# Two cross-attention layers on one core: the last two batch entries drained together, four orders changed in the repeated step

## The reference

```python
# layer 0, 16 heads of 16: only the context rows within 1 of each token's index count
q = split(rmsnorm(x, gamma_q) @ Wq.T); kn = rmsnorm(ctx, gamma_kv)
k, v = split(kn @ Wk.T), split(kn @ Wv.T)
w = square(relu(einsum('bhqd,bhkd->bhqk', q, k) / 4)); w = where(mask, w, 0)
x = x + merge(einsum(w / maximum(w.sum(-1), 1e-6), v)) @ Wo.T
# layer 1, one head
q, k, v = gelu(x @ Wq + bq), gelu(ctx @ Wk + bk), gelu(ctx @ Wv + bv)
x = softmax(q @ k.T) @ v @ Wf + bf + x
out = (x - mean) * rsqrt(var + 1e-5) * ln_gamma + ln_beta
```

## Time and profile before

| | |
|---|---|
| median of 3 runs | 367.44 us (366.91 to 369.47) |
| profiled execution | 368.78 us, of which the profile's span is 367.0 us |
| PE busy | 339.8 us, 93% |
| VectorE busy | 309.7 us, 84% |
| ACT busy | 246.3 us, 67% |
| POOL busy | 179.8 us, 49% |
| time of the chain that ended last | PE 66%, DVE 10%, ACT 9%, POOL 8% |
| mean granted clock of PE | 0.974 of 2.4 GHz |

### The profile page before, as it was taken

How to read it: one execution, slowest core, us unless ns; L and a number is a source line. 1 busy time by engine, 2 the same in 40 slices (tenths; PEclk the granted TensorE clock), 3 DMA queues, 4 the chain that set the end, 5 groups by cost and what they waited for, 6 DMA issues and landing times.

```text
span 367.0 us, 5550 instructions
## 1 busy us (share of the span) xinstructions
PE 339.8 (93%) x1904; PEld 241.2 (66%) x1904; DVE 309.7 (84%) x486; ACT 246.3 (67%) x491; POOL 179.8 (49%) x218
## 2 busy tenths in 40 slices
PE   3989998999999999999999999999999999978871
PEld 1565767767676767676767676767676767656740
DVE  0879696999998989998999999999999999895635
ACT  3797423477777686868686868686959595838542
POOL 3715020026565655556564747473838383636153
PEclk9989999999999999999999999999999999998985
DMA  7965625804141413132323232222222321101003
GB/s 245 325 193 143 198 67 127 246 2 142 57 144 58 143 60 136 65 126 75 117 84 114 86 108 94 101 96 95 91 102 81 101 89 49 59 0 57 2 0 114
DMA packets 21946, 38.48 MB, mean 105 GB/s; under 512 B 2144, under 2 KB 8288, under 8 KB 21920
## 3 DMA queue, kind: packets, MB, share of 16 engines
q1 hardware_dynamic: 18800, 29.48, 25.3%
q0 software_dynamic: 2160, 7.87, 6.2%
q10 hardware_dynamic: 960, 0.79, 0.7%
HBM read 17.29 MB, written 8.39 MB: 70 GB/s over the span
## 4 chain that ended last, share of the span: by engine, by line
PE 66%; DVE 10%; ACT 9%; POOL 8%; issue 7%; ACTq 0%; POOLq 0%
PE ps L440 9%; PE ps L442 8%; PE ps L441 8%; PE ps L519 8%; PE ps L485 6%; ACT bufs L880 4%; PE ps L675 4%; PE ps L569 4%; PE ps L491 4%; PE ps L684 4%; DVE stats L1111 4%; PE ps L600 4%; PE ps L574 2%; POOL rstd L379 2%; PE ps L472 1%
## 5 line engine op out<-in xcount | busy, mean ns | idle before, releaser
L1042 DVE TENSOR_TENSOR qkp<-ps,bufs 128x1024 f32<-128x1024 f32 x48 | 55.8, 1213 | 2.4 <-PE ps L485 2.4
L350 POOL TENSOR_TENSOR x_lo<-x_ring,x_hi 128x1024 fp32r<-128x1024 f32 x16 | 38.3, 2395 | 39.8 <-ACT x_hi L842 39.8
L389 POOL TENSOR_TENSOR bufs<-bufs,lng_row 128x1024 f32<-128x1024 f32 x15 | 36.1, 2404 | 36.9 <-ACT bufs L880 34.9
L918 ACT ACTIVATE xp_hi<-bufs 128x512 fp32r<-128x512 f32 x30 | 18.9, 632 | 50.5 <-DVE bufs L1122 50.5
L1053 DVE TENSOR_TENSOR ps<-ps,wn 128x1024 f32<-128x1024 f32 x32 | 39.2, 1224 | 2.8 <-PE ps L491 2.8
L363 POOL TENSOR_TENSOR mean_gap<-stats 128x4 f32<-128x4 f32 x14 | 2.8, 197 | 71.1 <-DVE stats L1111 71.1
L391 POOL TENSOR_TENSOR bufs<-bufs,lnb_row 128x1024 f32<-128x1024 f32 x15 | 35.6, 2374 | 1.2
L519 PE MATMUL ps<-qkp,cst 128*32 128x512 f32 x192 | 30.7, 598 | 0.4 <-DVE qkp L1042 0.4
L519 PE MATMUL ps<-bufs,cst 128*32 128x512 f32 x64 | 30.5, 598 | 0.0
L880 ACT ACTIVATE bufs<-ps,nbias,rstd 128x256 f32<-128x256 f32 x56 | 28.5, 568 | 2.7 <-POOL nbias L380 2.4
L440 PE MATMUL ps<-xp_hi,wh_q 128*128 128x512 f32 (+1 forms) x68 | 27.6, 405 | 2.6 <-DVE xp_lo L1125 1.9
(11 more groups left out here) (205 smaller groups left out, 925.8 us busy)
## 6 DMA issues: line engine op xcount, KB each, us to landing
x_ring<-xT SPq DMA_DIRECT2D x16, 512.0 KB, 3.5
out<-bufs POOLq DMA_DIRECT2D x15, 512.0 KB, 3.5
idx_ring<-idx SPq DMA_DIRECT2D x16, 256.0 KB, 4.0
wkv_lo<-kv SPq DMA_DIRECT2D x32, 126.0 KB
kvs<-kv SPq DMA_DIRECT2D x30, 126.0 KB
vfd<-bufs SPq DMA_DIRECT2D x8, 256.0 KB, 4.1
qkp<-ctxT SPq DMA_DIRECT2D x2, 512.0 KB, 7.3
bufs<-ctx SPq DMA_DIRECT2D x2, 512.0 KB, 8.7
```

Of the source, the lines that this page charges most:

```text
L350: G.tensor_tensor(x_lo[:, :, :], x_ring[:, e % RING, :, :], f32_view(x_hi[:, :, :]), ALU.subtract).then_inc(xl_ready, 2)
L389: G.tensor_tensor(zo, zn, lng_row[:, :].unsqueeze(1).broadcast_to([P, TT, D]), ALU.mult).then_inc(zg_ready, 1)
L1042: V.tensor_tensor(qk[:, s, :, :], ps[:, bank0:bank0 + 2, :], q0, ALU.mult).then_inc(qk_ready, 1)
```

## The change

**In the repeated step.** POOL no longer doubles `half_rstd` into `rstd`; ACT scales with `half_rstd`, `nbias` uses half of the shift's factor, and gamma is doubled once (`lng_twice`). ACT normalises all four tiles before it copies the second half of q0 (it did two, the copy, two). PE makes the second queries from the half `c = 1` first and waits for each half's rounding apart. PE starts the scores when the first half's gelu is done. These last two waits were one wait for both halves each.

**In the drain.** The step's loop ends one step earlier (`s` = 16). A list written out by hand takes its place and the old drain's: entry 14 (`OLD`) and entry 15 (`LAST`) alternate. The last picked values of 15 stand ahead of 14's second queries; 15's third product and sum are done in halves in VectorE (`half_third`); the halves of 15 use buffers and PSUM banks of their own and stand among 14's scores, exponentials and outputs. Products of the halves do their high parts first and wait for the remainder only then. POOL makes the remainder of half 1, VectorE rounds half 1. The scores of a half are packed as two tiles of 64 by 128, with one transpose each. The norms of 14 and 15 come last: statistics by VectorE; for 15, VectorE subtracts the mean and multiplies gamma in PSUM, then scales and adds beta; for 14, ACT normalises, then POOL does gamma and beta of one pair of tiles and VectorE those of the other, whose normalised rows stay in PSUM. SP issues four transfers of 256 KB. ACT's table loads are forced early by a one-element activation.

```diff
@@ gpsimd, norm_factors and scale_rows
-                G.tensor_scalar(nmean2[:, :], mean2[:, :], -1.0, None, ALU.mult).then_inc(mean_ready, 1)
+                G.tensor_scalar(nmean2[:, :], mean2[:, :], -0.5, None, ALU.mult).then_inc(mean_ready, 1)
-                G.tensor_tensor(rstd[:, :], half_rstd[:, :], half_rstd[:, :], ALU.add).then_inc(nbias_ready, 1)
+                    G.tensor_tensor(lng_twice[:, :], lng_row[:, :], lng_row[:, :], ALU.add).then_inc(twice_ready, 1)
@@ gpsimd, after the loop
+            norm_factors(OLD - 1)
+            scale_rows(OLD - 1)
+            write_rows(OLD - 1)
+            half_remainder(1)
+            final_power(0)
+            final_bias(0)
+            final_power(1)
+            final_gamma(0, 0)
+            final_beta(0, 0)
@@ tensor, step
-                    for c in range(DC):
-                        product(ps[:, Q1_BANKS[i], :], *weight("q1", c, i), xp_hi[:, c, :], xp_lo[:, c, :], c == 0, c == DC - 1, q1_mm)
+                    for c in (1, 0):
+                        if i == 0:
+                            pe.wait_ge(xph_ready, 2 * b + (2 - c))
+                            pe.wait_ge(xpl_ready, 2 * b + (2 - c))
+                        product(ps[:, Q1_BANKS[i], :], *weight("q1", c, i), xp_hi[:, c, :], xp_lo[:, c, :], c == 1, c == 0, q1_mm)
-                    pe.wait_ge(xph_ready, 2 * b + 2)
-                    pe.wait_ge(xpl_ready, 2 * b + 2)
@@ scalar, step (the two halves of normalise)
                 if n is not None:
                     normalise(range(2, TT))
+                if n is not None:
+                    normalise(range(0, 2))
                 if a is not None and f is not None:
...
                     copy_q0(a, 1)
-                if n is not None:
-                    normalise(range(0, 2))
@@ vector, after the loop: the product of a half, and the norm
+            def half_third(h):
+                dve.wait_ge(vg_mm, 3 * LAST + 3)
+                V.tensor_tensor(ps[:, 2 + h, :].rearrange("p (x d) -> p x d", d=HD), ps[:, 2 + h, :].rearrange("p (x d) -> p x d", d=HD),
+                                wn[:, CENTRE, 2 * h:2 * h + 2, :].rearrange("p j h -> p (j h)").unsqueeze(2).broadcast_to([P, 2 * H, HD]),
+                                ALU.mult).then_inc(half_prod, 1)
+                dve.wait_ge(half_prod, h + 1)
+                dve.wait_ge(sum_ready, 2 * LAST + 1)
+                V.tensor_tensor(att_flat(0)[:, h, :], ps[:, 2 + h, :], att_flat(1)[:, h, :], ALU.add).then_inc(half_sum, 1)
+            def final_centred(m, h):
...
+                    last = V.scalar_tensor_tensor(z, z, fin_nmean_t[:, m, j:j + 1], lng_row[:, :], ALU.add, ALU.mult)
+            def final_scaled(m, h, k):
...
+                    last = V.scalar_tensor_tensor(fin_rows_t[m][:, j, :], z, fin_rstd_t[:, m, j:j + 1],
+                                                  lnb_row[:, :], ALU.mult, ALU.add)
```

More of the change, by code:

```diff
@@ L754, in half_output, with old_queries @@
[L754 to L760 removed]
+                        product(ps[:, O0_BANKS[i], :], *weight("o0", c, i), o_hi[:, c, :], o_lo[:, c, :], c == 0, c == DC - 1, xp_mm)
+            def old_queries(i):
+                for c in (1, 0):
+                    pe.wait_ge(xpl_ready, 2 * OLD + (2 - c))
+                    product(ps[:, Q1_BANKS[i], :], *weight("q1", c, i), xp_hi[:, c, :], xp_lo[:, c, :], c == 1, c == 0, q1_mm)
@@ L766, in _, with half_high @@
                 t.then_inc(half_turn, 1)
-            older_transposed(LAST - 1)
-            half_project(0)
-            older_output(LAST - 1)
-            half_project(1)
-            half_queries(0)
-            half_queries(1)
+            def half_high(name, outs, hi, h, shared):
+                for i in range(DC):
+                    for c in range(DC):
+                        w_high, w_low = weight(name, c, i)
+                        mm(outs[i], w_high, hi[:, c, half_rows(h)], start=(c == 0 and not (shared and i)), stop=False, skip_group_check=True)
+                        mm(outs[i], w_low, hi[:, c, half_rows(h)], start=False, stop=False, skip_group_check=True)
@@ new lines, in half_low, with projected, queried @@
+            def half_low(name, outs, lo, h, done):
+                for i in range(DC):
+                    for c in range(DC):
+                        w_high, w_low = weight(name, c, i)
+                        t = mm(outs[i], w_high, lo[:, c, half_rows(h)], start=False, stop=(c == DC - 1), skip_group_check=True)
+                    t.then_inc(done, 1)
+            def projected(h):
+                return [ps[:, HALF_O0[h], i * 2 * P:(i + 1) * 2 * P] for i in range(DC)]
+            def queried(h):
+                return [ps[:, HALF_Q1[h][i], 0:2 * P] for i in range(DC)]
@@ L939, in _, with table, exps @@
             steps(step)
-            act.wait_ge(nmax_ready, LAST)
-            for j in range(TT):
-                A(ex[:, j, :], sc_rows[:, j, :], ACT.Exp, bias=nmax[:, j:j + 1],
-                  accum_out=ssum[:, j:j + 1]).then_inc(ex_ready, 1)
-            for h in range(2):
+            def table(function, k):
+                A(warm[:, k:k + 1], minus_half[:, 0:1], function)
+            def exps(n, rows_in, rows_out, tiles):
+                act.wait_ge(nmax_ready, n + 1)
+                for j in tiles:
+                    A(rows_out[:, j, :], rows_in[:, j, :], ACT.Exp, bias=nmax[:, j:j + 1],
+                      accum_out=ssum[:, j:j + 1]).then_inc(ex_ready, 1)
@@ L962, in _, with half_exp @@
-            for h in range(2):
+                    A(q1T_last[:, e, half_rows(h)], ps[:, HALF_Q1[h][e], 0:2 * P], ACT.Gelu, bias=vec[:, 2, e:e + 1]).then_inc(half_q1, 1)
+            def half_exp(h):
                 act.wait_ge(half_nmax, h + 1)
```

561 lines of the change are left out of this document (391 added, 170 removed).

## The result

The changed kernel takes **351.6 us** (median of 4 runs, 351.49 to 353.48), the kernel before beside it 367.2. The ratio is 0.958, 95% interval 0.952 to 0.963. The forecast was 356.3 and its range 352.5 to 361.5: the direction was right, the gain is 4.7 us larger than forecast, 0.9 beyond the range.

What follows compares the result with a forecast made beforehand. The prediction took VectorE's loop through PE's projection to bound the step, and engines waiting for each other the end. 367.44 - 3.7 (middle) - 8.4 (end) + 1.0 (clock) = 356.3 us; range 352.5 to 361.5.

Steps and rivals of the forecast that it cites:

- the term of the middle: Repeated step: VectorE's loop loses only its 0.28 wait for the maxima, step 18.72 to 18.44, so -3.7 us over 13 steps.
- POOL's removal: Repeated step: without POOL's doubling, nbias comes 0.7 or 0.16 us earlier; either will do, the sum is the same.
- The end: Drain: the rewritten order of the last two entries shortens the end of the kernel by 8.4 us.
- POOL's pow: Drain, norm of entry 15: POOL's power takes 1.04 us, done while VectorE is at the first four of eight passes.
- the 2.8 for the transfer: End of the drain: the span ends 2.8 us after the last VectorE pass, as before.
- clock +1.0: Drain: short PE pieces on the path at the lower clock add 1.0 us, taken between 0 and 2.
- The tables: Drain: each ACT table load costs 1.28 us; by the skill's page, three switches would add about 4 us.
- The middle gains PE's whole row: Rival, repeated step: all 7.1 us of PE's weight-load waits for ACT's rows are gained, giving 352.9 us; chance 0.08.
- The middle doesn't gain: Rival, repeated step: another VectorE wait replaces the one for the maxima, only the end gains, 360.0 us; chance 0.14.
- An early fall of the clock: Rival, drain: PE's clock falls early, some 2 to 6 us of slower work show, 358 to 362 us; chance 0.12.
- The slower case: Rival, repeated step: late nbias makes ACT hold back q0's copy and the loop; 372 us at 1.35 delay; chance 0.03.
- TensorE's wait for `x_hi(0)`: Sign, drain: ACT's x_hi(0), behind two exponentials, is PE's only longer wait, 0.4 us.

Runs made afterwards that it cites:

- before_reduce_2: The kernel before with two more reductions over constants in VectorE's step, ahead of the wait for the maxima's scores; 368.0 us, ratio 0.999.
- norm_only: The kernel before with one change: ACT normalises all four tiles before it copies the second half of q0; 362.5 us, ratio 0.982.
- pool_only: The kernel before with one change: POOL's doubling gone, gamma doubled once; 364.1 us, ratio 0.987.
- middle_only: The kernel before with the four changes of the repeated step alone and the old drain; 359.2 us, ratio 0.971.
- pick_behind: The changed kernel with TensorE picking entry 15's last rows behind entry 14's second queries again; 352.5 us.
- one_more_matmul: The changed kernel with one more 512-column matmul a step, its result overwritten; 355.0 us, ratio 0.958.

## Why the prediction was wrong, and where it was right

**The step that failed** is the term of the middle: "VectorE's loop has lost only the wait at L1151: 18.72 - 0.28 = 18.44. What is late next is VectorE's work; PE gets the slack", so 13 x 0.28 = 3.7. Measured were 7.1 (18.69 to 18.15). The prediction had the right number in hand, "its own floor would be 18.1", and gave that case 8 in 100. The loop was read as closed through VectorE, and VectorE's slack as the idle time written beside its wait. VectorE's loop does set the new step, as the prediction said, but at 18.15 and not at 18.44; it didn't set the old one. The slack was larger, for two reasons that the starts show and that no row of waits lists:

- Consecutive VectorE instructions overlap by 0.10: the next starts 1.13 after a pass of 1.22 (272.72 to 273.85). Where there is a wait, this overlap is lost too. Before, the maxima started 1.52 after the pass ahead (279.07 to 280.59), so 0.39 was free, of which 0.29 is printed.
- The sum was handed to TensorE at once, or so the loop assumed. Before, L569 started at 282.34, 0.20 after the sum's end at 282.14 (280.93 + 1.21); now it is 0.05. TensorE was then still at its own row ahead, whose last matmul starts 0.5 before L569 in both kernels (281.81, and 274.92). Another 0.15.

The starts are in these rows of the kernel before, VectorE's timeline and then PE's:

```profile
279.07 1.22 DVE L1053 TENSOR_TENSOR ps<-ps,wn 128x1024 f32<-128x1024 f32 x1
...
280.93 1.21 DVE L1080 TENSOR_TENSOR qkp<-ps,qkp 128x1024 f32<-128x1024 f32 x1
```
```profile
272.94 0.61 PE L485 MATMUL ps<-onehot,kv 128*128 128x512 f32 x2
273.51 0.47 PE L440 MATMUL ps<-xp_hi,wh_q 128*128 128x512 f32 x1
273.81 0.39 PE L441 MATMUL ps<-xp_hi,wl_q 128*128 128x512 f32 x1
...
275.85 0.39 PE L440 MATMUL ps<-xp_hi,wh_q 128*128 128x512 f32 x1
...
281.81 0.59 PE L519 MATMUL ps<-bufs,cst 128*32 128x512 f32 x1
282.34 1.09 PE L569 MATMUL ps<-cst,qkp 128*128 128x128 f32 x8
```

Together 0.54, which is the gain of the step. before_reduce_2, with 0.59 of work put there at no price that shows, says that it was free. The same rows say where the old step did lose time. Ahead of the transposes TensorE's distance is 0.53 in both kernels, so it never stood for VectorE's sum. The distances that shrank are those to the second queries (273.51 and 273.81: 0.57 and 0.30, now 0.45 and 0.23) and to and behind the UP keys (0.54 and 0.57, now 0.23 and 0.47), 0.60 in all, less some 0.05 that the next starts take longer. So the old step was set by the loop through these places: TensorE's projection, VectorE's residual, ACT's `xp_hi`, the normalised rows, TensorE's UP keys. norm_only and pool_only, which change only ACT's order and POOL's factors (with gamma), bear it out. The change shortened this loop until VectorE's was the longer.

**What each step change gives**, by the runs: ACT's order 0.36 to 0.39 alone (0.42 when taken out of the new step), POOL's doubling 0.13 to 0.16 alone (0.11), the queries' order 0.14, gelu's wait 0.04, within the noise. The prediction costed POOL's removal as either 0.7 or 0.16 earlier and said that either will do. POOL's timeline in the middle step of the kernel after, the line that follows the power, and then the line that stood behind the doubling before:

```profile
265.53 0.75 POOL L399 TENSOR_TENSOR nbias<-nmean,half_rstd 128x4 f32<-128x4 f32 x1
```
```profile
272.58 0.20 POOL L380 TENSOR_TENSOR nbias<-nmean,half_rstd 128x4 f32<-128x4 f32 x1
```

The multiplication took over the long time, so `nbias` comes only 0.14 earlier: it ends 0.89 after the doubling's start before (271.89 to 272.78) and 0.75 after its own start now. That is what pool_only and pool_old show. The Trainium skill, "GPSIMD Engine Reference", Specifications, says that GpSimd's SBUF interface is shared with VectorE and contended when a VectorE instruction has two SBUF inputs. The trace agrees: whichever POOL instruction starts with VectorE's subtraction (265.54) is the long one.

**The end** was 9.2, against 8.4 less 1.0 for the clock. In the trace before's time (8.07 later than after's, by the first transpose of the last step, 319.82 and 311.75), the halves' sums were ready at 332.7 and 334.0 (forecast 332.6, 333.9), `x_hi(0)` at 338.6 (338.6), the output of 14 at 346.0 (346.1), the second exponentials at 346.2 (346.3). VectorE's chain from there was shorter: it turns to 15's statistics at 348.4, not 349.0, since 14's six small factors take 0.50 from the first start to the next statistics, where they were taken at 0.73; the second six take 0.55. The first four of its eight passes start 1.58 ahead of the next (0.395 each, forecast 0.40), POOL's pow was hidden, the 2.8 for the transfer held. The term **clock +1.0** measured 0 in the pieces on the path: both outputs of 15 ran in 0.70, at full clock. Its source was also misread: the 2.07 of L757 is four matmuls, not two, and the same four take 1.13 at full clock, so the clock's share of it was 0.94. That makes 0.8 + 1.0 = 1.8 of the miss.

**The tables**: the loads took 1.28 each with nothing behind them, as the sum had it. The Trainium skill, "ScalarE: Activation LUTs", What ACT_TABLE_LOAD costs, has some 2.66 us for load and drain. Here 1.30 lies between the start of the load and the exponential (328.18 to 329.48), so the measurement decides against the page for this case.

**The rivals.** "The middle gains PE's whole row", 7.1, is what happened by the number; its 352.9 is 1.3 above the measured time. That the gain equals that row is chance: the row counts the weight loads' waits, of which 1.8 are left, while the matmuls' starts gained 0.41 a step at the UP keys and 0.19 at the second queries. "The middle doesn't gain" is refuted by middle_only. An early fall of the clock didn't come in any of the ten profiles with the new drain, not even with the 1.35 of pick_behind. The slower case needed a delay of POOL; none came. Of the signs named, TensorE's wait for `x_hi(0)` came (0.28 at 330.54), but not as the only one: it also waits 0.37 to 0.60 in five other places from 314 on.

The terms of the miss: middle 3.4, end 0.8, clock 1.0, and 1.0 by which the start was shorter, are 6.2 by the two spans. The spans differ by 17.3 and the medians by 15.8 (367.44 and 351.6), 1.5 less, which leaves the 4.7 by which the forecast was off.

## What to carry to other kernels

An engine's slack in a repeated step is the distance between starts, wait included, less what the same pair takes where nothing waits, plus the time that its result lies unused at the other end; the idle time beside a wait is only part of it. When two loops close within 0.5 us of each other, compute both lengths to the end and weigh both, and a probe that adds a known 0.3 or 0.6 to one engine tells which one binds, if the steps of its profile are read: one_more_matmul's total alone would have named TensorE here. The place where the other engine's starts move apart names the loop too. Slack belongs to a place and not to an engine: in the new step VectorE still waits 0.26 for TensorE's projection (L1320, at 264.93) and 0.23 for ACT's sums (275.63), and yet 0.33 more ahead of its maxima cost 0.35. When two engines' limits come as close as here, within 0.1 of 18.15, work taken from one alone has little left to give; whether those two waits could go, no run tried.

## What the hardware showed that was not expected

- A table load starts ahead of the wait of the function that it belongs to: at 328.18, 0.93 before the maxima that the exponential needs (329.11), with no activation there to force it. The trace of the kernel before has it too (279.76 against 281.01).
- TensorE's granted clock in the start differs from execution to execution of one kernel: over 20 to 30 us it was 0.83 in one profile of the kernel before and 1.00 in the other. The first `mean_gap` starts at 81.2 to 81.8 in the twelve profiles with full clock there, and at 82.3 to 84.3 in the five without. That is up to 3 us that no edit explains. Not all of it is clock: in the three latest (83.6 to 84.3) TensorE's wait for `kv` already ends at 24.0 to 24.5, ahead of the fall, and in all others at 22.3 to 23.0.
- After the same wait of 1.9 in the same drain the clock fell 1.5 us later (330.63), 10 us later with waits of 1.04 and 1.11 between, or not at all (before_reduce_2, with the same waits of 1.04 and 1.12).
- The 0.74 of one POOL instruction isn't its own: with it gone, the next took 0.75.
